# Attention and feed-forward block: where `bout` is added, and how the hinge sums enter the output product

## What is computed

```python
x = _layernorm(x + attention(x))          # sparsemax over 32 patterns, 16 heads
# feed-forward, M = 64 hidden units, INNER = 16 hinges for each
s = einsum('btd,dm->btm', x, Win) + bin_
h = relu(s[..., None] * W1 + b1)
g = einsum('btmh,mh->btm', h, W2) + b2
x = _layernorm(x + einsum('btm,md->btd', g, Wout) + bout)
```

## Time and profile before

| | before |
|---|---|
| median of 3 executions | 1397.43 us |
| the profiled execution, its own time | 1396.98 us |
| its span, first to last instruction | 1395.2 us |
| granted TensorE clock, mean over the span | 0.970 |
| PE, ACT, DVE, POOL busy | 93%, 84%, 79%, 47% |

### The profile page before, as it was taken

How to read it: one execution, slowest core, us unless ns; L and a number is a source line. 1 busy time by engine, 2 the same in 40 slices (tenths; PEclk the granted TensorE clock), 3 DMA queues, 4 the chain that set the end, 5 groups by cost and what they waited for, 6 DMA issues and landing times. The chain is left out here.

```text
span 1395.2 us, 28156 instructions
## 1 busy us (share of the span) xinstructions
PE 1298.3 (93%) x7118; PEld 854.7 (61%) x7118; DVE 1108.5 (79%) x4547; ACT 1167.7 (84%) x2640; POOL 660.7 (47%) x1642
## 2 busy tenths in 40 slices
PE   6981989999999999999999999999999999999974
PEld 5650566666676666666666666666766666554442
DVE  2986887898888888888888888888888888754554
ACT  2660756789999999999999999999999999988883
POOL 1330333345555555555455555555555554545544
PEclk9995999999999999999999999999999999999995
DMA  5380786555565555555555655655655555577743
GB/s 180 90 216 12 175 232 205 182 182 173 191 206 178 200 204 176 204 197 177 209 190 181 212 183 189 212 179 192 207 177 200 195 181 201 186 237 257 249 118 72
DMA packets 91849, 258.33 MB, mean 185 GB/s; under 512 B 15731, under 2 KB 15731, under 8 KB 75286
## 3 DMA queue, kind: packets, MB, share of 16 engines
q1 hardware_dynamic: 91670, 256.39, 56.6%
HBM read 206.00 MB, written 50.33 MB: 184 GB/s over the span
## 5 line engine op out<-in xcount | busy, mean ns | idle before, releaser
L619 PE MATMUL bank<-G_sb,pT 128*128 128x512 f32 x1024 | 460.7, 593 | 0.0
L619 PEld LDWEIGHTS bank<-G_sb,pT 128*128 128x128 f32 x1024 | 184.9, 191 | 183.4 <-issue 183.4
L1041 DVE SCALAR_TENSOR_TENSOR acc<-hinge,w2c,acc 128x512 f32<-128x512 f32 x224 | 167.6, 748 | 107.5 <-ACT hinge L734 107.3
L999 DVE MAX8 top<-bank 128x8 f32<-128x32 f32 x2048 | 212.5, 182 | 38.8 <-issue 38.7
L431 POOL TENSOR_TENSOR shift_sq<-sum,per_row_sq 128x1 f32<-128x1 f32 x256 | 89.3, 349 | 248.7 <-DVE y_sb L893 248.5
L734 ACT ACTIVATE hinge<-s_sb,b1c,w1c 128x512 f32<-128x512 f32 x256 | 206.0, 808 | 0.0
L548 PE MATMUL bank<-A_hi,xT_lo 128*128 128x512 f32 x512 | 203.7, 398 | 0.0
L546 PE MATMUL bank<-A_hi,xT_hi 128*128 128x512 f32 x512 | 203.6, 398 | 0.0
L547 PE MATMUL bank<-A_lo,xT_hi 128*128 128x512 f32 x512 | 203.4, 397 | 0.0
L719 ACT ACTIVATE unread<-y_sb,shift_sq 128x512 bf16<-128x512 f32 x256 | 184.0, 719 | 18.7 <-POOL minus_mean L433 18.7
L893 DVE SCALAR_TENSOR_TENSOR y_sb<-bank,y_sb 128x512 f32<-128x512 f32 x256 | 169.2, 663 | 13.4 <-PE bank L646 13.1
(11 more groups left out here) (119 smaller groups left out, 2536.7 us busy)
## 6 DMA issues: line engine op xcount, KB each, us to landing
G_sb<-G_of_heads SPq DMA_DIRECT2D x128, 1024.0 KB, 5.4
x_sb<-in_L_attn_query_dram SPq DMA_DIRECT2D x128, 256.0 KB, 4.7
y_sb<-in_L_attn_query_dram SPq DMA_DIRECT2D x256, 128.0 KB, 5.4
out_dram<-o_sb SPq DMA_DIRECT2D x256, 128.0 KB, 4.7
G_of_heads<-y_sb SPq DMA_DIRECT2D x64, 256.0 KB, 3.9
y_sb<-in_L_attn_Wk_dram SPq DMA_DIRECT2D x1, 1024.0 KB, 5.6
y_sb<-in_L_attn_Wq_dram SPq DMA_DIRECT2D x1, 1024.0 KB, 8.4
y_sb<-in_L_attn_Wv_dram SPq DMA_DIRECT2D x1, 1024.0 KB
```

Source lines behind the costliest of these rows:

```text
L619: mm = nc.tensor.matmul(o_ps[i % 2][:], pT[:, bass.ds(pair_place(turn, i) + (i % H * C + c) * P, P)], G_sb[:, i % GR, c, :], start=(c == 0 ...
L999: mx = nc.vector.max(top8[:, h, :], z_ps[i % 2][:, h * S:(h + 1) * S])
L1041: nc.vector.scalar_tensor_tensor(acc[:], hinge[:, k % HR, :], w2c[:, k:k + 1], acc[:], ALU.mult, ALU.add).then_inc(s_acc, 1)
```

## The change

- `bout` is loaded as 128 equal rows (`bout_bc`), and POOL adds it to `y_sb` (one 128x512 add a tile, in slot i + 27, once the tile has been transposed: `LAG_BOUT`). The pass for it and its two fp32r rows go. DVE's residual of the second norm waits for that add (`s_yb`) in place of the transposition.
- The two half sums are added ahead of the product. ACT copies the upper half of `acc` down to the lower partitions (`both`), POOL adds the lower half to it, ACT copies the sum into the lower half of `split` as fp32r (the hi part), POOL subtracts and writes the lo part into the upper half of `split`. With hi and lo in one operand, two passes (against `Wout_hi` and `Wout_lo`) take the place of three.
- For the last group the hinges are made four a slot in two slots, not two a slot in four, the add and the subtraction are DVE's, and the result lies in a tile of its own (`last_split`).
- In the drain: DVE takes the normalisation into `y_sb` and the copy of the transposed y from ACT; `s` goes to the bank of the x transpositions (tiles 102 and up), so that L604 no longer waits for the copies of `s`; and the output product of every second tile from 110 on uses the bank of the probabilities, so that it no longer waits for DVE's residual of the tile ahead.

```diff
+LAG_BOUT = 27
# POOL, in slot(), behind the two norm() and ahead of the two mean()
-                if in_range(turn, j, LAG_SPLIT) and (j - LAG_SPLIT) % GROUP == 0:
-                    pool.wait_ge(s_acchi, group_of(turn, i) + 1)
-                    nc.gpsimd.tensor_tensor(acc_lo[:], acc[:], acc_hi[:].bitcast(F32), ALU.subtract)...
+                lead = split_lead(turn, j)
+                if lead is not None and lead != LAST:
+                    pool.wait_ge(s_upper, lead // GROUP + 1)
+                    nc.gpsimd.tensor_tensor(both[0:M, :], acc[0:M, :], both[0:M, :], ALU.add).then_inc(s_both, 1)
+                    pool.wait_ge(s_hi, lead // GROUP + 1)
+                    nc.gpsimd.tensor_tensor(split[M:P, :], both[0:M, :], split[0:M, :].bitcast(F32),
+                                            ALU.subtract).then_inc(s_lo, 1)
+                    pool.wait_ge(s_lo, lead // GROUP + 1)
+                if in_range(turn, j, LAG_BOUT):
+                    pool.wait_ge(s_yT, base + i + 1)
+                    nc.gpsimd.tensor_tensor(y_sb[:, i % YR, :], y_sb[:, i % YR, :], bout_bc[:],
+                                            ALU.add).then_inc(s_yb, 1)
# PE
-                        pe.wait_ge(s_sc, 4 * (base + i))
+                        pe.wait_ge(s_yTc, base + i)
+                        if s_place(base + i - 1) is ys_ps:
+                            pe.wait_ge(s_sc, 4 * (base + i))
...
-                    nc.tensor.matmul(f_ps[:], pick_c[:], bout_rows[:], start=True, stop=False)
-                    nc.tensor.matmul(f_ps[:], acc_hi[:, here], Wout_hi[:], start=False, stop=False)
-                    nc.tensor.matmul(f_ps[:], acc_hi[:, here], Wout_lo[:], start=False, stop=False)
-                    nc.tensor.matmul(f_ps[:], acc_lo[:, here], Wout_hi[:], start=False, stop=True).then_inc(s_f, 1)
+                    nc.tensor.matmul(f[:], parts[:, here], Wout_hi[:], start=True, stop=False)
+                    nc.tensor.matmul(f[:], parts[:, here], Wout_lo[:], start=False, stop=True).then_inc(s_f, 1)
# ACT, ahead of the count (L770)
-                    act.wait_ge(s_acc, (group_of(turn, i) + 1) * KH)
-                    nc.scalar.copy(acc_hi[:], acc[:]).then_inc(s_acchi, 1)
+                    act.wait_ge(s_acc, (lead // GROUP + 1) * KH)
+                    nc.scalar.copy(both[0:M, :], acc[M:P, :]).then_inc(s_upper, 1)
# ACT, behind the normalisation into y_sb (L784) and ahead of L792
+                lead = split_lead(turn, j)
+                if lead is not None:
+                    act.wait_ge(s_both, lead // GROUP + 1)
+                    if 0 < lead < LAST:
+                        act.wait_ge(s_f, lead)
+                    nc.scalar.copy(split_of(lead)[0:M, :], both[0:M, :]).then_inc(s_hi, 1)
-                if in_range(turn, j, LAG_Y):
+                if in_range(turn, j, LAG_Y) and not vector_finishes(turn):
...
-                if in_range(turn, j, LAG_YT):
+                if in_range(turn, j, LAG_YT) and not vector_finishes(turn):
# DVE, in slot(): ahead of and behind the residual of the second norm
+                if split_lead(turn, j) == LAST:
+                    ... wait s_upper, add both; wait s_hi, subtract into last_split
+                if in_range(turn, j, LAG_YT) and vector_finishes(turn):
+                    ... copy ys_ps into yT
+                if in_range(turn, j, LAG_Y) and vector_finishes(turn):
+                    ... tensor_scalar y_sb (behind the one into o_sb)
```

More of the change, by code:

```diff
@@ L254, in vector_finishes, with s_place, f_place, hinges @@
             return isinstance(turn, int) and turn >= TILES // UNROLL
+        LAST = TILES - GROUP
+        ALONE_S = TILES - LAG_YT
+        ALONE_F = TILES + UNROLL - LAG_OUT
+        def s_place(i):
+            return xT_ps if i >= ALONE_S else ys_ps
+        def f_place(i):
+            return uT_ps if i >= ALONE_F and i % 2 else f_ps
+        def hinges(turn, j, half):
+            n = turn * UNROLL + j - LAG_HINGE
+            lead, q = n - n % GROUP, n % GROUP
+            if 0 <= lead < LAST:
+                return [(lead, 2 * q + half)]
+            if lead == LAST and 2 * q < GROUP:
+                return [(lead, 4 * q + 2 * half), (lead, 4 * q + 2 * half + 1)]
+            return []
+        def split_lead(turn, j):
+            n = turn * UNROLL + j - LAG_SPLIT
+            if n == LAST - 2:
+                return LAST
+            return n if 0 <= n < LAST and n % GROUP == 0 else None
+        def split_of(lead):
+            return last_split if lead == LAST else split[:]
         def so_far(turn, j, lag):
@@ L723, in make_hinge @@
             def make_hinge(turn, j, half):
-                i = j - LAG_HINGE
-                lead = i - i % GROUP
-                if not in_range(turn, 0, -lead):
-                    return
-                base, g, k = turn * UNROLL, group_of(turn, lead), 2 * (i % GROUP) + half
-                if k == 0:
-                    act.wait_ge(s_sc, 4 * (base + lead + GROUP))
-                if not isinstance(turn, int) or base + lead > 0 or k >= HR:
-                    act.wait_ge(s_acc, g * KH + k - HR + 1)
-                nc.scalar.activation(hinge[:, k % HR, :], s_sb[:, (lead // GROUP) % 2, :], ACT.Relu,
-                                     bias=b1c[:, k:k + 1], scale=w1c[:, k:k + 1]).then_inc(s_hinge, 1)
+                for lead, k in hinges(turn, j, half):
+                    g = lead // GROUP
+                    if k == 0:
+                        act.wait_ge(s_sc, 4 * (lead + GROUP))
+                    if lead > 0 or k >= HR:
+                        act.wait_ge(s_acc, g * KH + k - HR + 1)
+                    nc.scalar.activation(hinge[:, k % HR, :], s_sb[:, g % 2, :], ACT.Relu,
+                                         bias=b1c[:, k:k + 1], scale=w1c[:, k:k + 1]).then_inc(s_hinge, 1)
             def slot(turn, j):
@@ L1025, in hinge_step @@
             def hinge_step(turn, j, half):
[L1027 to L1042 removed]
+                for lead, k in hinges(turn, j, half):
+                    g = lead // GROUP
+                    dve.wait_ge(s_hinge, g * KH + k + 1)
+                    if k == 0:
+                        if lead > 0:
+                            dve.wait_ge(s_both, g)
+                        nc.vector.tensor_scalar(acc[:], hinge[:, k % HR, :], w2c[:, k:k + 1], b2c[:],
+                                                ALU.mult, ALU.add).then_inc(s_acc, 1)
+                    else:
+                        dve.wait_ge(s_acc, g * KH + k)
+                        nc.vector.scalar_tensor_tensor(acc[:], hinge[:, k % HR, :], w2c[:, k:k + 1],
+                                                       acc[:], ALU.mult, ALU.add).then_inc(s_acc, 1)
             slots(dve, slot)
```

86 lines of the change are left out of this document (44 added, 42 removed).

## The result

The changed kernel takes 1418.96 us (1417.94 to 1420.14) against 1397.72 for the kernel before on the same chip: ratio 1.0154, 95% interval 1.0137 to 1.0172. It is 21 us slower where 1381 and a gain of 16 were forecast, and it lies above the range (1350 to 1406).

What follows compares the result with a forecast made beforehand. PE was taken to bound the cruise (38.28 us a group, ACT next at 36.15), with no engine full in the drain. 1397.4 - 21 (cruise) + 4 (drain) + 1 (end) = 1381 us, range 1350 to 1406.

Steps and rivals of the forecast that it cites:

- DVE: nothing charged: Cruise: POOL's adds fall beside DVE's reads of PSUM, and DVE has 4.9 us a group to spare, so no cost.
- The criterion: Cruise: turns between POOL and DVE decide only from 1.0 us of hold for each new wide POOL instruction on.
- The third rival: Cruise: POOL and DVE take turns, DVE needs 39.8 us a group, 1439 us in all; chance 0.06.
- PE's two passes: Cruise: two passes a tile go, 1.9 us a group less, so PE needs 36.4 us a group.
- ACT's need: Cruise: one ACT instruction goes and two copies come, so ACT goes from 36.15 to 36.7 us a group.
- ACT's wait for `mean` in a split slot: Cruise: in a split slot ACT stands 0.5 us at its first L719 until POOL's `mean` is there.
- The half add and the subtraction: POOL's add of the two halves and its subtraction take 1.30 us each.
- The addition alone: POOL's add of `bout` to y takes 1.30 us, bounds 1.05 and 1.4.
- The drain's loop: Drain: an ACT and POOL chain gives plain slots of 5.5 us, split slots of 10.1, a group of 26.6 against 25.1.
- The entry of the drain: First drain slots: 128 and 129 take 6.2 and 6.6 us, split slots 130 and 134 take 10.6 and 10.4.
- the fourth rival: Drain: PE's clock stays low, a group takes 42.6 us in place of 26.6, 1469 us in all; chance 0.06.
- The end: Slots 151 to 162: 44.2 us after the change for 43.4 before, 1 us more, bounds 3 either way.

Runs made afterwards that it cites:

- e3: The changed kernel with bout left out altogether, added neither by POOL nor by PE: 1364.0 us, ratio 0.9762 to the kernel before.
- e1: The changed kernel without POOL's addition of bout, which is again a pass of PE: 1377.0 us, ratio 0.9865 to the kernel before.
- e2: The kernel before with POOL's addition of bout alone, PE's pass for it gone, halves not added: 1385.8 us, ratio 0.9923.
- e13: e10, but POOL adds bout for two tiles of four, the others get a pass of PE: 1362.3 us, ratio 0.9754 to the kernel before.
- e7: The changed kernel with POOL's addition of bout moved behind the two means in POOL's order: 1390.9 us, ratio 0.9954 to the kernel before.
- e10: The changed kernel, POOL adding bout for three tiles in four, behind the means (PE passes otherwise and in the drain), DVE finishing y from slot 131: 1372.6 us.
- e8: The changed kernel with a POOL memset of 128 x 1472 in place of the addition, bout left out: 1386.2 us, ratio 0.992 to the kernel before.

## Why the prediction was wrong, step by step

**The step that failed** is "DVE: nothing charged". It had the right rule and the right row (L939 beside L473) and assumed the place: "the adds fall beside DVE's reads of PSUM as I place them". Three of a group's four fell beside `cum`, `twice` and `differs`, and made DVE so late that the half-sum instructions met `twice` and `u_sb`. DVE was busy 35.65 us a group over the cruise for 32.48 in e3: 3.2 us, which PE and ACT then waited for. The trace of before could have told the place, since the addition was to stand between POOL's last norm (L449) and its `mean` (L431). Timelines of POOL and DVE there:

```profile
691.59 0.35 POOL L449 TENSOR_TENSOR shift<-minus_mean,rstd 128x1 f32<-128x1 f32 x1
694.37 0.19 POOL L431 TENSOR_TENSOR shift_sq<-sum,per_row_sq 128x1 f32<-128x1 f32 x1 [2.43 <-DVE y_sb L893]
...
692.73 0.15 DVE L909 TENSOR_TENSOR differs<-count 128x4 f32<-128x4 f32 x1
```

An addition of 1.30 us from 691.94 on has `differs` in its time.

**The criterion failed too.** The third rival had the mechanism, but let it decide only where DVE would be full, at 1.0 us of hold for each of five wide instructions, 4.9 us a group, and priced it at 39.8 us a group. It decided with 3.2 us a group, with DVE idle for 2.9: the idle time lies elsewhere in the order (1.3 us at the check's branch, 1.2 at the hinges). A late DVE instruction reached PE through `differs` and ACT through `acc` at once. Spare time of a group is no cover for a delay at one place.

**Right:** PE's two passes, 0.94 us a group for one pass a tile (e1, e2), and with two passes and half of the `bout` passes 36.87 (e13), where 36.4 + 0.47 was due. ACT's need, 36.7 forecast, 36.8 in e3. ACT's wait for `mean` in a split slot, 0.5 forecast, 14.4 / 23 = 0.63. The half add and the subtraction, 1.30 forecast, 1.28 and 1.27. The addition alone, 1.30 forecast: 1.27 in e7, 1.48 in the mean in the changed kernel, where it meets DVE.

**The drain's loop** was right in its chain: plain slots of 5.31 us (5.5 forecast) and split slots of 9.93 (10.1), a group of 25.86 for 26.6. In a split slot ACT waits 1.38 us for the half sum and 3.02 for `mean` (1.4 and about 3 forecast). e3 takes the addition out of the chain, and the group is 24.1.

**The entry of the drain** was the second miss: slots 127 to 139 were forecast at 82.4 us (the slots given there) and took 95.4. e3 tells 6.1 of it to the addition. Slot 129, forecast at 6.6, took 11.4: DVE still has the scores and the count to do and got y and its transposed copy on top. Timelines of ACT, DVE and PE in slot 129 of the kernel after:

```profile
1208.93 0.63 ACT L865 ACTIVATE side<-u_raw 128x512 bf16<-128x512 f32 x1 [4.30 <-DVE sum_above L973]
...
1204.71 1.69 DVE L1107 SCALAR_TENSOR_TENSOR acc<-hinge,w2c,acc 128x512 f32<-128x512 f32 x1
...
1210.29 0.33 PE L680 MATMUL bank<-yT,Win_sb 128*64 128x64 f32 x3 [3.62 <-DVE yT L996]
```

The `acc` of 1.69 us takes 0.73 elsewhere; it begins 0.24 us behind an addition of POOL and ends 0.54 behind its end. ACT stood for 4.3 us and PE for 3.6, and then the clock fell, the fourth rival in small. Windows of slots 130, 132 and 133 of the kernel after:

```profile
1211.83:1223.59 11.76, 10.90 (x47) 6.24 (x47) 8.69 (x17) 7.11 (x17) 9.45 (x17) 0.71 0.26 86
...
1229.06:1235.05 5.99, 3.57 (x9) 2.01 (x10) 4.46 (x11) 4.27 (x12) 4.24 (x11) 0.50 0.45 155
1235.05:1241.90 6.85, 6.85 (x38) 3.82 (x37) 4.33 (x9) 4.78 (x12) 4.93 (x12) 0.96 0.46 157
```

What the fall costs is seen at slot 136, of which e1 and e3 have the same work but for one pass (windows of e1, then of e3):

```profile
1228.10:1233.25 5.15, 5.15 (x32) 2.90 (x31) 4.10 (x9) 4.19 (x10) 3.95 (x11) 1.00 0.61 212
```
```profile
1214.99:1222.67 7.68, 7.68 (x33) 3.57 (x32) 4.36 (x10) 4.28 (x10) 3.97 (x11) 0.80 0.36 127
```

With a granted clock of 0.80 (0.50, that is 1.2 GHz, in its first 3.0 us, then 2.4 GHz) in place of 1.00 and PE in all of it, the slot is 2.5 us longer; PE had stood for 2.7 us in the slot ahead, where the fall began. In the loop of the kernel after the slack of the chain covers the falls: slot 151 takes 5.31 us at a granted clock of 0.50, slot 149 the same at 1.00. Over the entry the granted clock is 0.91 in the kernel after, 0.96 in e10 and 1.00 in the kernel before. Even e10 takes 84.7 us to slot 139. How the entry divides between clock and chain was not tried and stays open.

**The end** was forecast at 44.2 us and took 45.9; without the addition it is 44.0.

## What to carry to other kernels

Before work is moved to POOL, lay its wide instructions beside DVE's program, instruction by instruction, at the place in the order where they will stand: one of 1.3 us holds even the smallest DVE instruction of the kinds below that comes in its time, and those that other engines wait for cost the most. Two changes that are gains alone can lose together, as here, where ACT had 1.1 us a group to spare with the addition alone and none with both: after taking work from the engine that bounds, work out the slack of the next one anew. Where a price hangs on the place, moving the instruction past its next neighbours (28 us here) or leaving it out of one more slot in four (10 us, e10 to e13) is worth a trial before the idea is dropped.

## What the runs showed of the hardware

- A DVE instruction that reads two operands from SBUF, or a `tensor_scalar` from SBUF to SBUF, and that begins while POOL's two-input instruction runs, is held to the end of it in these traces, whatever its size. In the kernel after `differs` (128x4) began within L516 in all 23 cases and ended 0.01 to 0.03 us behind it, `twice` (128x16) in 23 cases 0.02 to 0.04 behind, `cum` (128x128) in 21 cases 0.15 behind. `u_sb` (128x512), beside the subtraction L510, ended 0.55 behind that in 23 cases. It goes both ways: L516 took 1.26 us at least and up to 1.87. Not held: `sum_side` and `sum_above` (reductions, 0.41 us each time), L1092 and L1039 with an input in PSUM (0.69 and 0.68). The Trainium skill (GPSIMD Engine Reference, 8. Key points) names DVE instructions in a two-port mode or with two SBUF inputs as those that contend. The trace agrees for two SBUF inputs, with `differs` held from 0.15 to 1.14 us; in which mode `twice` ran no row shows.
- A memset on POOL holds less: timelines of DVE and POOL in e8, where `differs` and `twice` both fall into it.

```profile
644.29 0.15 DVE L966 TENSOR_TENSOR differs<-count 128x4 f32<-128x4 f32 x1
...
645.02 0.47 DVE L976 TENSOR_SCALAR twice<-sum_side 128x16 f32<-128x16 f32 x1
```
```profile
644.13 1.33 POOL L518 MEMSET unused<- 128x1472 f32 x1
```

- Half of the partitions cost POOL the same: 1276 and 1268 ns for 64x512, 1300 for 128x512; and ACT too, 0.62 us for a copy of 64x512 as for L758 with 128.
